# Half of the narrow products behind each up round, and the next expert's transposes between the two halves of the down products

## The reference

```
T = 32 * 65 tokens, H = 192, E = 128 experts, 6 chosen for a token, CAP = 192 places, I = 464
xb  = x[token_buf].reshape(E, CAP, H)                 # the rows of each expert's tokens
gu  = einsum('ech,ehf->ecf', xb, W_gate_up)           # up products, gate and up
g,u = split(gu, 2);  inter = silu(g) * u
yb  = einsum('eci,eih->ech', inter, W_down)           # down products
yb  = yb * w_buf                                      # weight of the token for this expert
routed = zeros(T, H).at[token_buf].add(yb)            # added to the token's row
```

## Time and profile before

| what | value |
|---|---|
| median of 3 runs | 936.86 us (936.58 to 936.96) |
| profiled execution | 934.52 us |
| its span, first to last instruction | 932.7 us |
| TensorE (PE) busy | 830.9 us, 89% |
| weight loads (PEld) | 731.8 us, 78% |
| VectorE (DVE) busy | 722.6 us, 77% |
| ScalarE (ACT) busy | 345.7 us, 37% |
| GpSimd (POOL) busy | 307.7 us, 33% |
| experts' loop on TensorE | 731.73 to 917.60 us |
| mean granted clock of TensorE | 0.970 |

### The profile page before, as it was taken

One profiled execution on the slowest core, in us unless ns is written; L12 is line 12 of the kernel. 1 busy time (PEld: TensorE's weight loads), 2 busy tenths in 40 slices (PEclk: granted clock), 3 DMA queues, 4 the chain that ended last, 5 costly groups with the idle time before them and its releaser, 6 DMA issues.

```text
span 932.7 us, 22271 instructions
## 1 busy us (share of the span) xinstructions
PE 830.9 (89%) x7603; PEld 731.8 (78%) x7603; DVE 722.6 (77%) x3781; ACT 345.7 (37%) x971; POOL 307.7 (33%) x354
## 2 busy tenths in 40 slices
PE   1687899899899899899899999999999999999993
PEld 1576688788788788888789989998879767676762
DVE  3356899999899899999999979799675465656562
ACT  0335554544544544545445344432210122222220
POOL 7021213403313223224123131121121276766664
PEclk8699999999999999999999999999998899999997
DMA  7410000101101101001001100010112466666651
GB/s 222 117 52 1 2 27 23 40 17 37 30 17 36 30 11 39 17 24 34 26 23 44 31 6 21 22 45 20 45 28 64 112 160 144 160 144 160 144 129 24
DMA packets 48231, 54.25 MB, mean 58 GB/s; under 512 B 9013, under 2 KB 41531, under 8 KB 48108
## 3 DMA queue, kind: packets, MB, share of 16 engines
q1 hardware_dynamic: 39180, 43.89, 16.4%
q0 software_dynamic: 6352, 7.62, 5.6%
q10 hardware_dynamic: 2608, 1.60, 0.7%
HBM read 42.40 MB, written 10.69 MB: 57 GB/s over the span
## 4 chain that ended last, share of the span: by engine, by line
DVE 48%; PE 38%; issue 5%; ACT 4%; SPq 2%; DVEq 1%; POOL 0%; DMA 0%; ACTq 0%; POOLq 0%
DVE b_arena L1500 9%; PE p_big L999 3%; PE p_shared L831 3%; DVE b_top_a L1486 3%; PE p_big L686 3%; PE p_shared L832 3%; PE p_big L687 2%; DVE b_top_d L1486 2%; PE p_shared L837 2%; DVE b_arena L1548 2%; DVE b_top_b L1486 2%; DVE b_top_c L1486 2%; PE p_small L693 2%; DVE b_rstd L1238 2%; PE p_big L1004 2%
## 5 line engine op out<-in xcount | busy, mean ns | idle before, releaser
L1769 POOL DMA_INDIRECT b_arena<-x_rows,b_index x44 | 68.0, 1544 | 49.4 <-DVE b_index L1565 36.6
L686 PE MATMUL p_big<-b_xT,b_ff1a 128*128 128x128 f32 x384 | 77.5, 285 | 1.4 <-ACT b_xT L1029 1.4
L1703 POOL TENSOR_TENSOR b_arena<-b_kY,b_mask_k 64x256 f32<-64x256 f32 x16 | 9.7, 608 | 205.9 <-ACT b_kY L1054 205.9
L687 PE MATMUL p_big<-b_xT,b_ff1b 128*128 128x128 f32 x384 | 76.5, 282 | 0.0
L1029 ACT COPY b_xT<-p_small 128x256 f32<-128x256 f32 (+1 forms) x97 | 35.4, 377 | 83.4 <-PE p_small L677 83.3
L1734 POOL TENSOR_TENSOR b_arena<-b_arena 128x768 f32<-128x768 f32 x16 | 27.0, 1687 | 117.8 <-DVE b_arena L1512 117.8
L686 PEld LDWEIGHTS p_big<-b_xT,b_ff1a 128*128 128x128 f32 x384 | 61.6, 200 | 2.5 <-ACT b_xT L1029 2.5
L999 PE MATMUL p_big<-b_xeT,b_arena 128*116 128x192 f32 x320 | 61.9, 336 | 0.0
L687 PEld LDWEIGHTS p_big<-b_xT,b_ff1b 128*128 128x128 f32 x384 | 60.7, 199 | 0.0
L720 PE MATMUL p_big<-b_arena,b_q_blk 128*128 128x256 f32 (+3 forms) x256 | 48.9, 334 | 12.5 <-ACT b_q_blk L1061 12.4
L720 PEld LDWEIGHTS p_big<-b_arena,b_q_blk 128*128 128x128 f32 x256 | 41.3, 190 | 19.4 <-POOL b_arena L1703 12.6
(11 more groups left out here) (379 smaller groups left out, 2548.1 us busy)
## 6 DMA issues: line engine op xcount, KB each, us to landing
b_arena<-in_w_gate_up SPq DMA_DIRECT2D x20, 464.0 KB
b_arena<-in_w_down SPq DMA_DIRECT2D x20, 336.0 KB
b_xp<-in_xp SPq DMA_DIRECT2D x16, 384.0 KB, 3.1
b_arena<-in_w_gate_up SPq DMA_DIRECT2D x40, 116.0 KB
xT_rows<-b_xmT SPq DMA_DIRECT2D x16, 128.0 KB, 1.8
b_xT_late<-xT_rows SPq DMA_DIRECT2D x16, 128.0 KB, 2.2
h_rows<-b_h SPq DMA_DIRECT2D x16, 96.0 KB, 1.6
x_rows<-b_xm SPq DMA_DIRECT2D x32, 48.0 KB, 2.0
```

Source lines behind the costliest of these rows:

```text
L686: mm(o, ff1a[:, c * 128:(c + 1) * 128], xTa[s][:], start=True, stop=False)
L687: last = mm(o, ff1b[:, c * 128:(c + 1) * 128], xTb[s][:], start=False, stop=True)
L1769: G.indirect_dma_start(xg[s][0:rows, h, :], None, x_rows[:, :], bass.IndirectOffsetOnAxis(index[s][0:rows, h:h + 1], 0)).then_inc(S(f"gath ...
```

## The change

The 34 narrow products are cut at h: the 17 of h = 0 stay behind up round 0 and the 17 of h = 1 go behind up round 1. The transposes of the next expert go behind the two wide down products of half 0. All four narrow down products come after the wide ones of half 1. On VectorE the index computation goes from round 0 to behind round 1's inner values; the value load, the copy of the column and the first compare stay in round 0 and so follow L1645 at once (the generator has one more stop, `early`, and is stepped twice). Work ahead of the loop is as before, ScalarE, GpSimd and SP too.

```diff
+            def slots_half(s, v, h):
+                if h == 0:
+                    pe.wait_ge(S("hot_ready"), v)
+                for t in range(NT):
+                    last = mm(lists_bank[s][:, 400 + 6 * h:406 + 6 * h], hot[s][:, t, 128 * h:128 * h + 128], rhs[s][:, t, :],
+                              start=(t == 0), stop=(t == NT - 1))
+                if h == 1:
+                    last.then_inc(S("index_mm"), 1)
+
             def slots_of(s, v):
...
+                slots_half(s, v, 0)
+                slots_half(s, v, 1)
...
                         last.then_inc(S(f"eup{r}"), 1)
-                        if r == 0:
-                            slots_of(s, v + 2)
-                    gathered(1 - s, 32 * i + 32 + 32 * s, v + 1)
+                        slots_half(s, v + 2, r)
                     pe.wait_ge(S("y_done"), v)
                     for r in range(2):
                         pe.wait_ge(S(f"einner{r}"), v + 1)
                         for c in range(2 * r, 2 * r + 2):
                             mm(aux[s][:, 0:D], einner[s][:, c, 0:128], w_dn[s][:, c, :], start=(c == 0), stop=False)
-                        for c in range(2 * r, 2 * r + 2):
-                            half = slice(64 * (c % 2), 64 * (c % 2) + 64)
-                            last = mm(aux[s][half, D:2 * D], einner[s][:, c, 128:CAP], w_dn[s][:, c, :],
-                                      start=False, stop=(c >= NIC - 2))
+                        if r == 0:
+                            gathered(1 - s, 32 * i + 32 + 32 * s, v + 1)
+                    for c in range(NIC):
+                        half = slice(64 * (c % 2), 64 * (c % 2) + 64)
+                        last = mm(aux[s][half, D:2 * D], einner[s][:, c, 128:CAP], w_dn[s][:, c, :],
+                                  start=False, stop=(c >= NIC - 2))
                     last.then_inc(S("down_mm"), 1)
...
-            def slots_of(j, s, v):
+            def slots_of(j, s, v, early=False):
...
+                if early:
+                    yield
                 dve.wait_ge(S("twice"), v)
...
-                    slots = slots_of(2 * i + s + 3, 1 - s, v + 3)
+                    slots = slots_of(2 * i + s + 3, 1 - s, v + 3, True)
...
                             ts(add_w[s][:], slot_w[s][:], 0.5, None, op0=ALU.mult).then_inc(S("kept"), 1)
-                            dve.wait_ge(S("kept"), v)
-                            indices_of(s, v + 2)
-                        if r == 0:
                             next(slots)
+                            next(slots)
+                    dve.wait_ge(S("kept"), v)
+                    indices_of(s, v + 2)
                     run(slots)
```

More of the change, by code:

```diff
@@ L922, in class_tile @@
                 yield from router(1, 1, B, xTa[1][:, 0:B], xTb[1][:, 0:B])
-            def slots_of(s, v):
[L925 to L930, removed]
+            def slots_half(s, v, h):
[6 more added lines that the diff above has]
+                    last.then_inc(S("index_mm"), 1)
+            def slots_of(s, v):
+                slots_half(s, v, 0)
+                slots_half(s, v, 1)
             def gathered(s, gather_value, v):
```

## The result

The changed kernel takes 922.25 us (921.25 to 922.58, 5 runs) against 936.96 (936.58 to 938.9) before: ratio 0.9842, 95% interval 0.9826 to 0.9858. I had said 927.8, in a range of 926.0 to 933.5. The sign and the mechanism held; the gain is 14.7 us where I had 9.1.

The account below looks back on a forecast made before the run. TensorE's own serial work plus its wait for VectorE's round-1 inner values was taken as the bound. Savings of 10.0 us less 0.93 at the end gave 9.1 off 936.86, so 927.8 us, range 926.0 to 933.5.

Parts of the forecast that it names:

- What bounds the kernel: TensorE idles in the expert loop only before the second half's down products, awaiting VectorE's inner values: 8.7 us over 20 experts.
- (c): VectorE's chain to round 1's inner values: value load runs ahead, TensorE can start at 6.91, 0.08 us before needed; no stall.
- (a): Half of TensorE's 34 narrow products moves behind up round 1, which ends at 5.08, not 5.51 us; switches cost 0.
- (b): Transposes move behind TensorE's first two wide down products, narrow ones come together last: 8.79 us per expert without a stall.
- (d): Index computation and GpSimd's gathers move later; rows land at 14.5 us, wanted at 15.15: median slack 0.7 us, cost 0.
- the stall of 0.1 us: By the shared port rule, VectorE's first compare waits 0.3 us for a scatter-add, stalling 0.1 us per expert; no own chance.
- (e): At the loop's end the last scatter starts 3.28 us behind the last product, before 2.35: 0.93 us added once.
- partial cover: Rival: round 1's inner values still late by value load or GpSimd's count, 0.23 us per expert, 932.4; 0.24 with dear switches.
- no effect: Rival: TensorE's order brings nothing and the stall stays at 0.4 us, about 936 to 938 us; chance 0.06.
- Switches: Rival: splitting and regrouping cost TensorE 0.1 us per expert, 2 us in all, 929.8; chance 0.24 with partial cover.
- late gather: Rival: gathered rows reach TensorE's transposes late, deciding from landing time 4.99 us; 940.9 us at 6.3; chance 0.10.

## Why the prediction was wrong

**What bounds the kernel**: right. The stall went, and with it its 0.39 to 0.48 us.

**(c) the chain and VectorE's run-ahead**: right. L1547 came 0.13 us behind L1652, the inner values reached TensorE at 6.92 where I had 6.91. The margin of 0.08 us turned out as a wait of 0.08, since TensorE came at 6.84 (by transposes of 0.58; the chain was as modelled, the blocks ahead of TensorE's arrival were shorter).

**(a) and (b), the sum of TensorE's blocks: the step that failed.** I put it that "the new order of switches costs between -0.07 and 0.1 us for an expert. I take 0, since there are as many switches as before." Counting switches was the error: what counts is which. The change has one change from wide to narrow down products in place of two. Each costs about 0.11 us at the end of the wide block (0.85 against 0.74) and 0.16 in the narrow one (0.80 for eight records against twice 0.48), and 0.05 in transposes that follow narrow ones. That is 0.32 us for an expert, of which 0.08 goes into the wait above and 0.02 into the hundredths of the other blocks: 8.57 and not 8.79, 4.4 us in all. The experiments without the grouping give 8.79 to the hundredth. The bounds of -0.07 to 0.1 us did not hold it: I took the 0.07 between two equal narrow blocks, which was indeed run-out (0.47 twice where no stall follows), for the size of a switch. In the earlier trace rows every wide down block stands ahead of a narrow one, so they could not show what a wide block takes without, and I did not ask. The runs show what a change of shape costs, not why.

**(d) the gathers**: the cost of 0 was right, with more slack than I had (1.8 us, from gathers of 1.0 us and a landing 3.4 us after the start).

The reading beside it was wrong. I compared the rows with what the Trainium skill says of a shared port pair (SBUF — State Buffer, section "SBUF: two separate sides") and wrote that the trace doesn't agree, as the gather takes "its 1.61 with VectorE's work beside it". The 1.61 was the lengthening: the earlier trace rows have 0.97 for the same line at 737.61. A gather that starts inside a compare waits for its end, as the rule has it for an engine that comes second. The other half of the rule isn't seen here: compares that start inside a scatter-add keep their 0.96 us, so the stall of 0.1 us that I worked out from it and set aside did not come.

**(e) the end**: wrong by its whole size, the second step that failed. It rested on a gather of 1.61 us, which was that of a gather inside a compare; with 1.02 and 0.93 the queue is free before the output is ready, and the end is as long as before (2.35).

Sum on the profiles: 9.1 + 4.4 + 0.9 = 14.4 us, where the two loops differ by 14.5 and the medians by 14.7.

**The rivals**: partial cover and no effect did not come. "Switches" was put on the wrong side of zero. The late gather did not come, but its price was mis-sized: with gathers really late the kernel lost some 25 us against before (12 to 30 over its runs).

## What to carry to other kernels

Read the time of a block of matrix products from the start of the next one, and ask what kind stands behind it: put products of one tile shape next to each other across the stages of a loop body, as far as the dependencies allow, and check the chains again, since the shorter blocks are also shorter cover. Where a wait feeds a control instruction such as a value load, moving the waiting work behind it lets the load run ahead for nothing. Keep TensorE's stalls short: 0.4 us cost 0.4, while 2.4 us cost 5. Before a duration is carried to another place in the loop, as my 1.61 us was, look what runs beside it there.

## What the runs showed of the hardware that I had not expected

- A change of tile shape in TensorE's stream costs 0.1 to 0.27 us (wide to narrow columns 0.11 + 0.16; deep to 64 rows 0.19 over two blocks, and 0.07 at the deep block ahead). The mechanism is not shown.
- A stall of 2.4 us in an expert's loop brings the granted clock to 0.74 on average, stalls of 0.4 us leave it at 1.00. In between both were seen: 1.11 us with 0.62 around it, 1.22 us with 1.00.
- A gather that starts inside a bf16 one-hot compare on VectorE ends 0.77 to 0.90 us behind the compare's end, up to 1.8 us in all; elsewhere it takes 0.90 to 1.11. A compare that starts inside a scatter-add keeps its 0.96 us.
- One set of 12 runs of an unchanged kernel came out 1.8% longer than its other three sets.
